# A four-block transformer kernel on one core: other banks, another order and another layout where block 1 meets the slots

## The reference, cut to what matters

```
def _L0_attn_ref(x, ...):            # block 1: 16 heads of 16 channels
    attn = softmax(alpha * (q @ k.T) * SCALE / TEMPERATURE + beta) * gamma
    out = attn @ (v * (1 + ka))      # ka: a small gate per head and channel
    return out @ Wproj + bproj
def _L0_ffn_ref(x, slot_query, ...): # block 2: 16 slots, 16 experts
    o = slot_query + mha(slot_query, x, x, d_Wq, d_bq, d_Wk, d_bk, d_Wv, d_bv, d_Wo, d_bo)
    h = layernorm(o) * e_lng + e_lnb                       # one slot for each expert
    y = (silu(h @ e_W1 + e_b1) * silu(h @ e_Wg + e_bg)) @ e_W2 + e_b2
    o = o + y
    return mha(x, o, o, c_Wq, c_bq, c_Wk, c_bk, c_Wv, c_bv, c_Wo, c_bo)
...
x = layernorm(x + _L0_attn_ref(x, ...))
x = layernorm(x + _L0_ffn_ref(x, ...))
x = layernorm(x + _L1_attn_ref(x, ...))                   # block 3, retention
x = layernorm(x + _L1_ffn_ref(x, ...))                    # block 4, local attention and feed-forward, twice
```

## Time and profile before

| | us |
|---|---|
| median of 3 runs (2560.79 to 2566.89) | 2562.2 |
| the profiled execution | 2562.65 |
| its span in the trace | 2560.8 |
| last L245 of block 1 begins | 629.26 |
| first matmul of the head stage begins | 734.48 |
| first matmul of the experts begins | 762.18 |

### The profile page before, as it was taken

The page is one execution under the profiler, slowest core; times in us unless marked ns, Lnnn a source line. Parts: engine busy times, 40 slices in busy tenths (PEclk is TensorE's granted clock), DMA queues, the critical chain, the costliest instruction groups (busy, mean ns, idle before and its releaser), DMA issues.

```text
span 2560.8 us, 42694 instructions
## 1 busy us (share of the span) xinstructions
PE 2334.7 (91%) x16381; PEld 1379.9 (54%) x16432; DVE 1663.7 (65%) x4331; ACT 1228.2 (48%) x2774; POOL 725.9 (28%) x717
## 2 busy tenths in 40 slices
PE   5899999998789798886889999999999999999997
PEld 2333333333552476665556666666666666666664
DVE  5777777775530275665787667766777677776753
ACT  2655555555222251110566565566556655565540
POOL 2232223220110131111443333333333333333311
PEclk7999999999899899997999999999999999999999
DMA  8233333332219502000000000000000000000001
GB/s 293 90 108 97 108 102 99 110 118 79 90 68 412 245 2 87 22 18 36 1 5 5 5 3 4 5 5 30 3 12 30 28 13 18 5 22 22 19 21 37
DMA packets 70970, 158.59 MB, mean 62 GB/s; under 512 B 6336, under 2 KB 48432, under 8 KB 63184
## 3 DMA queue, kind: packets, MB, share of 16 engines
q1 hardware_dynamic: 68464, 146.68, 16.3%
q0 software_dynamic: 2304, 9.18, 1.6%
HBM read 116.52 MB, written 35.13 MB: 59 GB/s over the span
## 4 chain that ended last, share of the span: by engine, by line
PE 70%; DVE 16%; ACT 4%; DMA 4%; issue 2%; POOL 2%; SPq 1%; another core or an unknown queue 0%; POOLq 0%; DVEq 0%; ACTq 0%
PE banks L1846 9%; PE banks L1824 6%; PE banks L1705 6%; PE banks L245 4%; PE banks L1719 4%; PE banks L213 4%; PE banks L221 3%; PE banks L1806 3%; PE banks L1325 3%; PE banks L1749 2%; PE banks L284 2%; PE banks L265 2%; PE banks L1764 2%; DVE arena L2355 2%; DMA arena<-in_e_Wg 2%
## 5 line engine op out<-in xcount | busy, mean ns | idle before, releaser
L439 DVE TENSOR_REDUCE arena<-banks 128x1 f32<-128x512 f32 x512 | 323.8, 682 | 113.1 <-PE banks L213 113.0
L354 ACT ACTIVATE arena<-banks 128x512 f32<-128x512 f32 x512 | 279.4, 595 | 165.6 <-PE banks L221 144.1
L1846 PE MATMUL banks<-arena 128*128 128x512 f32 x640 | 293.2, 594 | 6.3 <-DVE arena L2063 5.9
L1916 ACT ACTIVATE arena<-arena 128x256 f32<-128x256 f32 (+1 forms) x512 | 286.3, 562 | 3.4 <-DVE arena L2016 3.1
L2154 POOL TENSOR_TENSOR arena<-arena 128x512 f32<-128x512 f32 x128 | 162.8, 1272 | 401.3 <-DVE arena L2047 401.2
L1705 PE MATMUL banks<-arena 128*128 128x512 f32 x512 | 245.4, 602 | 5.7 <-DVE arena L2047 4.9
L213 PE MATMUL banks<-arena 96*128 96x512 bf16 x512 | 203.8, 400 | 20.5 <-DVE arena L439 12.4
L2150 POOL TENSOR_TENSOR arena<-arena 128x16 f32<-128x16 f32 x64 | 187.5, 2930 | 5.3
L1846 PEld LDWEIGHTS banks<-arena 128*128 128x128 f32 x640 | 116.5, 190 | 131.8 <-issue 119.6
L221 PE MATMUL banks<-arena 128*128 128x512 bf16 x461 | 175.6, 384 | 3.3 <-ACT arena L354 1.8
L1888 ACT ACTIVATE arena<-arena 128x256 f32<-128x256 f32 (+1 forms) x256 | 102.1, 471 | 154.4 <-DVE arena L1992 154.4
(11 more groups left out here) (302 smaller groups left out, 4421.4 us busy)
## 6 DMA issues: line engine op xcount, KB each, us to landing
arena<-in_e_W SPq DMA_DIRECT2D x32, 1024.0 KB, 12.1
arena<-stacks SPq DMA_DIRECT2D x64, 384.0 KB, 4.5
arena<-in_e_Wg SPq DMA_DIRECT2D x16, 1024.0 KB, 14.5
stacks<-arena SPq DMA_DIRECT2D x32, 384.0 KB, 2.5
stacks<-arena SPq DMA_DIRECT2D x32, 256.0 KB, 2.7
arena<-dens POOLq DMA_DIRECT2D x32, 256.0 KB, 4.5
arena<-in_xT SPq DMA_DIRECT2D x8, 512.0 KB, 9.0
stacks<-arena SPq DMA_DIRECT2D x32, 128.0 KB, 2.5
```

The costliest lines, as they stand in the source:

```text
L354: e.activation(ex[:, j], self.psum[:, 3 + k % 2], ACT.Exp).then_inc(s["a_e"], 1)
L439: e.tensor_reduce(mx[:, t, j:j + 1], self.psum[:, k % 3], AX.X, ALU.max, negate=True).then_inc(s["a_m"], 1)
L1846: i = e.matmul(bank, weights[:, c], self.hT[:, c], start=c == 0, stop=c == 1)
L1916: k = e.activation(pr[:, h, at:], pr[:, h, at:], ACT.Exp, bias=mx[:, h:h + 1], scale=rn[:, h:h + 1], accum_out=den[:, h:h + 1])
```

## The change

There are five edits.

1. The last 32 exponentials (units 30 and 31) go round five banks, 3, 4, 0, 1, 2, where they had two. A score matmul of these waits for the exponential four back (`a_e` k-4), and the first into banks 0 to 2 for the last maximum.
2. The jobs of `TAIL` share banks 7 and 6 in turn (6 is that of unit 31's sums, so `turn1` of sequence 6 waits for the copy of these).
3. `TAIL` is in another order: `gather` stands ahead of `apply`, slot step 0 ahead of the turns of sequence 6, slot step 3 ahead of `scale`, so that the four `proj` follow each other.
4. The bias `c_bo` is added to x by POOL after the slots, in one row of eight, behind the root of the slots' layer norm, and not once per slot step.
5. The head values are made with slots moving: 32 columns of `d_Wv` (16 of them the head's) are the weights, 128 slots move, four heads stand under each other in a bank and the result comes out turned. `d_Wo` and `d_bv` are laid out for that by the host with gaps, so the turn and copy between are gone; `d_Wo` is loaded in two halves, the second when sequence 7 is turned. `d_bo` and the slot query are added ahead of it; the normalisation is two instructions and not three; h is turned ahead of o; and four query products stand there, not six, which puts four in round 2 of the experts.

The diff, cut to its core:

```diff
+        self.misc_tail = Ring([7, 6], tail, self.misc.counts)
...
+    def exp_bank1(self, k):
+
+        late = (UNITS - LAG) * TILES * UNIT
+        return 3 + k % 2 if k < late else (3, 4, 0, 1, 2)[(k - late) % 5]
...
-                    if k >= 2:
+                    late = k - (UNITS - LAG) * TILES * UNIT
+                    if late >= 5:
+                        w.wait_ge("a_e", k - 4)
+                    elif late >= 2:
+                        w.wait_ge("a_m", 4 * TILES * UNITS)
+                    elif k >= 2:
                         w.wait_ge("a_e", k - 1)
...
+            elif self.misc_tail.place[use] == 1:
+                emptied = "a_out", UNITS
...
-TAIL = [("apply", 6, 0), ("gather", 7, 0), ("turn0", 6, 0), ("turn1", 6, 0), ("s", 0, 0), ("s", 1, 0), ("inverse", 7, 0), ("s", 2, 0), ("scale", 7, 0), ("scale", 7, 1),
-        ("proj", 7, 0), ("proj", 7, 1), ("s", 3, 0), ("proj", 7, 2), ("proj", 7, 3), ("norm", 7, 0), ("s", 4, 0), ("apply", 7, 0), ("s", 5, 0), ("turn0", 7, 0), ("turn1", 7, 0),
+TAIL = [("gather", 7, 0), ("apply", 6, 0), ("s", 0, 0), ("turn0", 6, 0), ("turn1", 6, 0), ("s", 1, 0), ("inverse", 7, 0), ("s", 2, 0), ("s", 3, 0), ("scale", 7, 0), ("scale", 7, 1),
+        ("proj", 7, 0), ("proj", 7, 1), ("proj", 7, 2), ("proj", 7, 3), ("norm", 7, 0), ("s", 4, 0), ("apply", 7, 0), ("s", 5, 0), ("turn0", 7, 0), ("turn1", 7, 0),
         ("s", 6, 0), ("s", 7, 0), ("s", 8, 0), ("s", 9, 0)]
+
+FIRST_QUERIES = 4
...
-        for hd in range(H2):
+
+        for g in range(4):
             for c in range(CHUNKS):
-                i = e.matmul(ps[:, 6, hd * 16:hd * 16 + 16], g3[:, c, hd], W["d_Wv"][:, c, hd * 16:hd * 16 + 16], start=c == 0, stop=c == 1)
+                for j in range(4):
+                    at = c * CH + (4 * g + j) * 16
+                    i = e.matmul(ps[32 * j:32 * j + 32, 6, g * P:(g + 1) * P], self.wv_d[:, at:at + 32], g3[:, c, 4 * g + j], start=c == 0, stop=c == 1, skip_group_check=True)
         i.then_inc(s["h_mm"], 1)
         self.tensor2_queries(e, w, (0,))
         w.wait_ge("h_v", 1)
-        for c in range(CHUNKS):
-            i = e.transpose(ps[:, 3, c * P:(c + 1) * P], self.tmp2[:, c * P:(c + 1) * P], self.ident)
+        for g in range(4):
+            i = e.matmul(ps[:, 0, 0:256], self.headsT[:, g], self.wo_d[g // 2][:, g % 2], start=g == 0, stop=g == 3)
         i.then_inc(s["h_mm"], 1)
...
+        self.tensor2_queries(e, w, (1, 2))
         w.wait_ge("h_v", 3)
...
-        unit = 6 + 4 * q + place
+        unit = FIRST_QUERIES + 4 * q + place
...
+        w.wait_ge("h_p", 1)
+        e.scalar_tensor_tensor(h, o, st[:, 6:7], S("e_lng"), ALU.subtract, ALU.mult).then_inc(own.up(), 1)
         w.wait_ge("h_p", 3)
...
+        e.scalar_tensor_tensor(h, h, st[:, 8:9], S("e_lnb"), ALU.mult, ALU.add).then_inc(s["h_v"], 1)
...
-    def gpsimd2_slot(self, e, w, n):
-        c = n - 2
-        if c >= 0:
-            w.wait_ge("s_take", c + 1)
-            e.tensor_tensor(self.x_nat[:, c], self.x_nat[:, c], repeated(self.S("c_bo"), TILES), ALU.add).then_inc(self.s["s_bias"], 1)
...
         w.wait_ge("h_p", 2)
         e.tensor_tensor(st[:, 8:9], st[:, 9:10], self.half[:, 0:1], ALU.pow).then_inc(s["h_p"], 1)
+        for b in range(SEQS):
+            e.tensor_tensor(self.x_nat[:, b], self.x_nat[:, b], repeated(self.S("c_bo"), TILES), ALU.add).then_inc(s["s_bias"], 1)
...
+        e.dma_start(self.wo_d[1], wo[:, 2:4]).then_inc(s["l_dw"], 16)
```

More of the change, by code:

```diff
@@ L172, in layout1 @@
         self.g_area = [g[:, 16 + i * P:16 + (i + 1) * P] for i in range(9)]
-        self.meet, self.const = split(r.take(512), CHUNKS, 256), r.take(16)[:, 0:2]
+        assert r.at <= self.END - 512
+        self.meet = split(self.arena[:, self.END - 512:self.END], CHUNKS, 256)
         once = self.sums[1]
@@ L186, in layout1 @@
                 uses += [x for x in self.at1[u, t] if x[0] in MISC]
-        uses += [x for x in TAIL if x[0] in MISC]
+        tail = [x for x in TAIL if x[0] in MISC]
         self.misc = Ring([7], uses, {
@@ L195, in steps1, with bank1 @@
                 yield u, t
+    def bank1(self, use):
+        return self.psum[:, self.misc_tail.bank(use) if use in self.misc_tail.place else self.misc.bank(use)]
+    def exp_bank1(self, k):
+        late = (UNITS - LAG) * TILES * UNIT
+        return 3 + k % 2 if k < late else (3, 4, 0, 1, 2)[(k - late) % 5]
     def tensor1(self, e, w):
@@ L251, in tensor1_task @@
             return
-        bank = self.psum[:, 7]
-        emptied = self.misc.emptied((kind, unit, index))
+        use = (kind, unit, index)
+        bank = self.bank1(use)
+        if use in self.misc_tail.place:
+            emptied = self.misc_tail.emptied(use)
+            if self.misc_tail.place[use] == 0:
+                last, unit_before, index_before = self.misc_last
+                name, per, first, step = self.misc.counts[last]
+                emptied = name, unit_before * per + index_before // step + first
+            elif self.misc_tail.place[use] == 1:
+                emptied = "a_out", UNITS
+        else:
+            emptied = self.misc.emptied(use)
         if emptied and emptied[0] == "a_gated":
@@ L369, in scalar1_task @@
     def scalar1_task(self, e, w, kind, unit, index):
-        s, S, bank = self.s, self.S, self.psum[:, 7]
+        s, S, bank = self.s, self.S, self.bank1((kind, unit, index)) if kind in MISC else None
         if kind == "qk":
@@ L494, in vector1_task @@
     def vector1_task(self, e, w, kind, unit, index):
-        s, own, bank = self.s, self.own1, self.psum[:, 7]
+        s, own, bank = self.s, self.own1, self.bank1((kind, unit, index)) if kind in MISC else None
         if kind == "qk" and unit < 2:
@@ L607, in gpsimd1 @@
                 self.gpsimd1_task(e, w, *task)
-        for kind, unit, index in TAIL:
-            if kind == "s":
-                self.gpsimd2_slot(e, w, unit)
-            else:
-                self.gpsimd1_task(e, w, kind, unit, index)
+        for task in TAIL:
+            self.gpsimd1_task(e, w, *task)
     def gpsimd1_task(self, e, w, kind, unit, index):
@@ L741, in layout2 @@
         wide = r.at
-        self.W2 = {n: split(r.take(512), CHUNKS, CH) for n in ("d_Wv", "d_Wo", "c_Wq", "c_Wk", "c_Wv", "c_Wo")}
+        wv, self.wo_d = r.take(512), [split(r.take(512), 2, CH)]
+        self.wv_d = self.arena[:, wide:wide + 512 + HD1]
+        self.W2 = {n: split(r.take(512), CHUNKS, CH) for n in ("c_Wq", "c_Wk", "c_Wv", "c_Wo")}
+        self.W2["d_Wv"] = split(wv, CHUNKS, CH)
         self.ring2_at = r.at
@@ L760, in layout2 @@
         r = Columns(self.arena, self.R + 22336, r.at)
+        assert r.end + 512 <= self.END - 512
+        self.wo_d.append(split(self.arena[:, r.end:r.end + 512], 2, CH))
         self.kblk = split(r.take(512), CHUNKS, SEQS, 32)
@@ L847, in tensor2 @@
         i.then_inc(s["h_mm"], 1)
-        self.tensor2_queries(e, w, (5,))
+        w.wait_ge("h_v", 2)
+        for c in range(CHUNKS):
+            i = e.transpose(ps[:, 5, c * P:(c + 1) * P], self.o2[:, c * P:(c + 1) * P], self.ident)
+        i.then_inc(s["h_mm"], 1)
+        self.tensor2_queries(e, w, (3,))
         hT = split(self.padded, CHUNKS, EXPERTS, 32)
@@ L993, in scalar2 @@
         s, ps = self.s, self.psum
-        self.scalar2_queries(e, w, range(6))
+        self.scalar2_queries(e, w, range(FIRST_QUERIES))
         hidT = split(self.hid2, 8, P)
@@ L1208, in sync2 @@
         w.wait_ge("a_st1", 48 * 16)
-        for n in ("d_Wv", "d_Wo"):
-            e.dma_start(self.W2[n], split(self.dram[n], CHUNKS, CH)).then_inc(s["l_dw"], 16)
+        wo = split(self.dram["d_Wo"], 4, CH)
+        e.dma_start(self.W2["d_Wv"], split(self.dram["d_Wv"], CHUNKS, CH)).then_inc(s["l_dw"], 16)
+        e.dma_start(self.wo_d[0], wo[:, 0:2]).then_inc(s["l_dw"], 16)
         for n in ("c_Wq", "c_Wk", "c_Wv", "c_Wo"):
@@ L2289, in layout @@
         self.pieces = {"keep": r.take(self.dram["keep"].shape[-1])}
-        self.half, self.ident16 = r.take(64), r.take(64).bitcast(BF16)
+        self.half, self.const, self.ident16 = r.take(48), r.take(16)[:, 0:2], r.take(64).bitcast(BF16)
         self.small_from = r.at
```

51 lines of the change are left out of this document (21 added, 30 removed).

## The result

The changed kernel takes 2523.2 us (median of 4 runs, 2520.81 to 2525.39) against 2563.2 us before on the same chip (4 runs, 2560.79 to 2566.89): ratio 0.9843, 95% interval 0.9826 to 0.9860, so 40.0 us less, where 35.5 were forecast. The profiled execution took 2520.81 us, with a span of 2519.0.

The account below looks back on a forecast made before the run. PE bounds until 629 us; then 132.9 us of DVE work, denominators' trip and head-stage chain before the experts, which wait for weights. Terms -3.3 - 14.6 + 3.4 - 6.4 - 14.6 = -35.5 from 2562.2 give 2527 us; range 2520 to 2537.

Parts of the forecast that it names:

- rival without a fall of the clock: PE's clock does not fall in the 4.9 us gap before the four `proj`: 3.4 us more won, 2523; chance 0.17.
- last exponentials: Last eight steps: five banks shorten four steps without a `proj` by 0.33 each, the others some 0.1; -1.6 us.
- from there to the first `proj`: Slot step 0 runs earlier; first `proj` of sequence 7 at 660.6, not 663.89: -3.3 with the exponentials' 1.6 within it.
- four `proj` in a row, with the half clock: Sequence 7: four `proj` at 1.8 each, 7.2 for 21.8 us, -14.6; half clock after PE's idle gap, +3.4.
- slot step 4 to the head stage: Slot steps after the `proj`: held products, restarts and the turn's wait for bank 7 go, 0.9 + 0.9 + 1.2 + 3.4 = -6.4.
- head stage: Between slot steps and experts: packed matmuls and two queries put off, 13.1 for 27.7 us, -14.6.
- experts: Experts start near 726.7, their stretch stays 110 us: 0. Rival that they swallow some: 3.6 to 8 back, chance 0.10.
- rival of a late trip: Reciprocals' trip is slow beside weight loads, `scale` starts at up to 662, not 657.7: +6, 2533; chance 0.08.
- held products: Slot steps: six DVE products held by POOL's bias addition, 1.47 against 0.49; PE's waits and restarts from them would go.
- rival of the low clock: Clock is low in the head stage too; 10 us of running there would cost 5: 2532; chance 0.15.
- Bias additions: Head stage: POOL's additions beside DVE's last normalising step cost 0, with 1.5 us of cover; bounds 0 and 0.8.
- a longer stretch: Experts: a stretch longer than 110 us was named as a sign that the forecast is wrong.

Follow-up runs that it names:

- the twelve others: The twelve follow-up kernels, each the changed kernel with one or several edits undone or added; measured medians from 2512.4 to 2539.6 us.

## Why the prediction was right

The forecast of 2527 was 3.8 us above the time, and the range held it. The rival without a fall of the clock had 2523, the measured time itself; that is chance, for the clock did fall. By the steps:

| step | forecast | measured |
|---|---|---|
| last exponentials | -1.6 | -1.3 |
| from there to the first `proj` | -1.7 | -1.8 |
| four `proj` in a row, with the half clock | -11.2 | -12.4 |
| slot step 4 to the head stage | -6.4 | -6.2 |
| head stage | -14.6 | -14.9 |
| experts | 0 | +1.5 |
| sum | -35.5 | -35.1 |
| unchanged code | 0 | -6.7 |

That the two sums differ by 0.4 only is partly luck: the four `proj` are 1.2 better than forecast and the experts 1.5 worse.

- **Exponentials.** The step of 2.55 measured 2.56. The steps with a `proj` gained almost nothing: four steps at 0.32 are the whole 1.3.
- **First proj.** Forecast at 660.6, it began at 657.33 in an execution that was 3.5 ahead by then, so at 660.8 in the time of the other. DVE waited 1.72 for the denominators where I had 0.5, and 0.51 for the reciprocals where I had none, but its slot steps 0 and 1 took 4.3 and not the 4.6 I gave them, so `scale` began at 658.0 in that time (654.45 and 3.5) for 657.7, and the idle time of PE came out at 5.37 for 4.9. The rival of a late trip was there in its first 0.5 us only.
- **Four proj.** The clock did fall, so the rival without that fall is out. The price was 2.4 and not 3.4 (with the gap filled the same work took 7.01), just under the low bound of my 2.5 to 4.8. That mis-sized term is the largest ahead of the experts. The bound itself was read too high: in the 4.9 behind the 4.20 of idle PE stood still for 0.78, so half of 4.1 was lost there, 2.0. And no single figure fits: the same place costs 1.5 to 2.8 from kernel to kernel.
- **Slot steps.** The total is right, but its parts are less so. The held products are worth 2.8 in waits, near the 3.0 of the forecast. One bank cost 2.4 in this stretch for the 3.4 that I read from the turn's wait. The remaining 1.0 belongs to both edits together. In the kernel before, DVE's copy for which the turn waited 3.17 stands behind a held product; with one bank and no bias additions beside it the turn waits 2.20. DVE before:

```profile
703.23 1.47 DVE L1075 TENSOR_SCALAR arena<-arena 128x512 f32<-128x512 f32 x1
...
705.21 0.68 DVE L521 COPY arena<-banks 128x512 f32<-128x512 f32 x1
```

- **Head stage.** The packed products took 1.96 for 2.15, query 2 waited 0.78 for its bank, and all was done in 12.78 for 13.1. The clock stayed at 1.00, so the rival of the low clock is out. With the old head stage behind the same slot steps it fell again, during the products with 16 columns, so the fall belonged to that stage and not to what came ahead of it.
- **Bias additions.** I took no cost, with bounds 0 and 0.8. The hold came (2.22 for 0.48, so 1.74) and used up the cover: PE asked for h 0.23 before it was there. Even that had no price, since query 3 behind the turns waits for bank 7, and PE gained nothing when h came earlier. The Trainium skill, GPSIMD Engine Reference, section 1 (Specifications), says that GpSimd contends with VectorE's instructions that have two inputs in the on-chip memory. The trace agrees with the rule: 2.22 for 0.48. The section gives no length for the hold; the 2.0 and the 0.8 in the prediction came from the rows of the held products. The 0.8 did not come, because it left out what the end of the stage waits for. Once query 2 waits for nothing and query 3 has its bank, the price is 1.5.
- **Experts.** Their stretch is 1.5 longer, of which ten matmuls at half clock behind a wait for weights are most: 3.47 at 816.15, for 1.90 in the earlier trace rows behind the like wait. The same stretch took 110.3 to 112.1 in the twelve others. I had named a longer stretch as a sign that the forecast is wrong; most of the 1.5 is no work or wait that the change brought there, but one more fall of the clock.

```profile
816.15 3.47 PE L894 MATMUL banks<-arena 128*32 128x512 f32 x10 [1.44 <-DMA arena<-in_e_Wg]
```

The other 4.9 us (40.0 between the medians, less 35.1) come from no step of the forecast. The stretches of unchanged code are 6.7 shorter between the two profiled executions, with 13.6 us less at half clock in them. The 3.5 ahead lie before anything that was changed, so at least that part is how the clock happened to fall in this execution. Whether a share of the part behind comes from how the change shifts the work against the clock was not settled: with 13 kernels that are equal there, it went both ways.

## What to carry to other kernels

Where a chain of short links sets the end, an idle time of PE can cost twice: once itself, and once for the clock behind it. Work that is ready and stands behind the wait should be moved ahead of it, and one should then look at once for who stands behind the moved work (`apply` behind slot step 5). A new order may pay more together with another bank or buffer (9.0 as against some 6.8 here), so the two are to be tried apart and together. An operation that is hidden is so by something in particular: name it, for the next edit may take it away, as the bank of query 2 did with the bias additions.
